# Swapping the two kinds of score products in TensorE's order, in the heads of an attention layer

## The reference

```python
q = _rope((x @ w_q.T) ...); k = _rope((x @ w_k.T) ...)     # 4 x 1024 tokens, 16 heads of 16
scores = jnp.einsum('bhqd,bhkd->bhqk', q, k) * SCALE
scores = jnp.where(tok_mask[None, None], scores, -jnp.inf)  # blocks of 64, causal
attn = jax.nn.softmax(scores, axis=-1)
ctx = jnp.einsum('bhqk,bhkd->bhqd', attn, v)
x = _layernorm(x + ctx @ w_o.T)
```

## Time and profile before

| | us |
|---|---|
| median of three runs | 1910.19 |
| lowest, highest | 1908.25, 1912.74 |
| the profiled execution's own time | 1904.56 |
| its span, first to last instruction | 1902.7 |

### The profile page before, as it was taken

How to read it: one execution, slowest core, us unless ns; L and a number is a source line. 1 busy time by engine, 2 the same in 40 slices (tenths; PEclk the granted TensorE clock), 3 DMA queues, 4 the chain that set the end, 5 groups by cost and what they waited for, 6 DMA issues and landing times.

```text
span 1902.7 us, 26419 instructions
## 1 busy us (share of the span) xinstructions
PE 1636.9 (86%) x10042; PEld 1007.7 (53%) x10043; DVE 1141.5 (60%) x2367; ACT 792.5 (42%) x1296; POOL 235.7 (12%) x237
## 2 busy tenths in 40 slices
PE   3899999986999964788899989899989899889797
PEld 3788888874558853333355433355433455433345
DVE  5556665647421144668558677568667578677465
ACT  5444444421212200437744157643167552177530
POOL 4333333311420001000000000100000100000100
PEclk8999999987999976759999989899989899988999
DMA  2000000005115502000000000000000000000000
GB/s 102 12 23 23 22 22 22 22 12 177 26 33 151 149 12 91 1 1 2 1 1 1 0 1 2 23 1 1 1 1 2 23 1 1 0 1 1 23 1 22
DMA packets 27147, 47.96 MB, mean 25 GB/s; under 512 B 7312, under 2 KB 16016, under 8 KB 26256
## 3 DMA queue, kind: packets, MB, share of 16 engines
q1 hardware_dynamic: 26464, 44.74, 7.4%
q0 software_dynamic: 576, 1.77, 0.3%
HBM read 37.59 MB, written 9.06 MB: 25 GB/s over the span
## 4 chain that ended last, share of the span: by engine, by line
issue 59%; POOL 2%; DVE 0%; POOLq 0%; DVEq 0%
POOL rs_sb L1310 1%; POOL ve_sb L1307 0%; POOL qks_sb L1325 0%; POOL v_sb L1324 0%; POOL qks_sb L1315 0%; DVE bn_sb L1489 0%; DVE x_sb_sb L1504 0%; POOLq L1144 0%; POOLq L65 0%; POOL qks_sb L1326 0%; DVE mv_sb L1495 0%; DVEq L1144 0%; POOL v_sb L1323 0%; DVEq L65 0%; DVEq L1493 0%
## 5 line engine op out<-in xcount | busy, mean ns | idle before, releaser
L1546 DVE TENSOR_REDUCE mx_sb<-s_ps 128x1 f32<-128x512 f32 (+1 forms) x512 | 313.0, 652 | 140.9 <-PE s_ps L1818 80.0
L1378 ACT ACTIVATE room_sb<-s_ps 128x1024 f32<-128x1024 f32 (+1 forms) x320 | 280.9, 950 | 21.6 <-PE s_ps L1842 20.5
L1815 PE MATMUL s_ps<-room_sb 48*128 48x512 f16 (+3 forms) x640 | 175.9, 345 | 25.1 <-DVE mx_sb L1546 16.8
L1862 PE MATMUL cm_ps<-room_sb,v_sb 128*32 128x512 f32 (+3 forms) x1536 | 167.4, 526 | 0.8 <-ACT room_sb L1384 0.8
L1842 PE MATMUL s_ps<-room_sb 51*128 51x128 f16 (+4 forms) x1152 | 123.5, 287 | 41.8 <-ACT room_sb L1378 34.9
L1307 POOL TENSOR_TENSOR ve_sb<-mv_sb,eps_sb 128x4 f32<-128x4 f32 x24 | 5.0, 210 | 1120.8 <-DVE mv_sb L1495 1120.8
L1985 PE MATMUL cm_ps<-w_fd_sb,room_sb 128*128 128x256 f32 x512 | 126.5, 394 | 14.7 <-DVE room_sb L1625 14.7
L1842 PEld LDWEIGHTS s_ps<-room_sb 50*128 50x128 f16 (+1 forms) x1152 | 39.1, 96 | 180.8 <-ACT room_sb L1378 145.0
L1815 PEld LDWEIGHTS s_ps<-room_sb 48*128 48x128 f16 x640 | 54.5, 97 | 145.8 <-DVE mx_sb L1546 97.1
L1972 PE MATMUL s_ps<-xbT_sb,w_fg_sb 128*128 128x512 f32 x256 | 128.9, 615 | 0.8 <-ACT xbT_sb L1415 0.8
L1972 PE MATMUL s_ps<-xbT_sb,w_fu_sb 128*128 128x512 f32 x256 | 127.1, 607 | 0.0
(11 more groups left out here) (242 smaller groups left out, 3250.1 us busy)
## 6 DMA issues: line engine op xcount, KB each, us to landing
we_gu_sb<-we_gu SPq DMA_DIRECT2D x32, 352.0 KB
we_dn_sb<-we_dn SPq DMA_DIRECT2D x32, 176.0 KB
x_in_sb<-x SPq DMA_DIRECT2D x9, 512.0 KB, 3.6
rows<-x_sb_sb SPq DMA_DIRECT2D x8, 512.0 KB, 3.0
x_sb_sb<-rows SPq DMA_DIRECT2D x2, 2048.0 KB, 11.5
out<-x_sb_sb SPq DMA_DIRECT2D x8, 512.0 KB, 2.6
xp_sb<-w_in SPq DMA_DIRECT2D x1, 1024.0 KB, 5.5
x_sb_sb<-w_up SPq DMA_DIRECT2D x1, 1024.0 KB, 6.6
```

The costliest lines, as they stand in the source:

```text
L1378: act.activation(weights[(g * NU + u) % SLOTS_P][:, 2 * pair:2 * pair + 2, 0:width(u) * P], W[s % 2][:, :, 0:width(u) * P], ACT.Exp, scale ...
L1546: dve.tensor_reduce(mx[:, pair, k % 2, slot:slot + 1], X[:, k % 2, 0:count * P], AX.X, ALU.max, negate=True).then_inc(mx_ok, 1)
L1815: last = pe.matmul(X[:, k % 2, at * P:(at + plain) * P], query[head:head + NORM, i * P:(i + 1) * P], key[head:head + NORM, j * P:(j + plai ...
L1862: last = pe.matmul(O[32 * h:32 * h + 32, (i - half * GT) * P:(i - half * GT + count) * P], v[:, j, g * HG + h, :], weights[(g * NU + u) % ...
```

## The change

In all steps but the first of a group, S(s + 1) used to come before M(s); now M(s) comes before S(s + 1). Step 0 had this order already. Nothing is added or removed, and no other engine's order is touched.

```diff
                         if s == 0 and g > 0:
                             weighted(b, g - 1, NU - 1, 0)
-                        if s == 0 and of < NHG:
+                        if of < NHG:
                             for_maxima(b, of, m, m + 2)
                         if s + 1 < STEPS:
                             scores(b, g, s + 1)
                         elif g + 1 < NHG:
                             scores(b, g + 1, 0)
-                        if s > 0 and of < NHG:
-                            for_maxima(b, of, m, m + 2)
                         if s == 1 and g > 0:
```

## The result

| | before | after |
|---|---|---|
| median us | 1908.99 (6 runs) | 1884.11 (6 runs) |
| lowest, highest | 1898.01, 1912.74 | 1880.26, 1888.07 |
| profiled span | 1902.7 | 1886.1 |
| mean granted clock of that execution | 0.922 | 0.927 |

The ratio is 0.9879, with a 95% interval from 0.9857 to 0.9902: 1.2% faster, some 23 us.

A forecast was written before the change was run, and what follows sets the result against it. In the heads TensorE and VectorE were taken to wait for each other, with ScalarE beside them. Gains of 1.5 + 0.3 + 0.25 us per block, times 4, made 8.2: from 1910.19 to 1902.0 us, range 1893 to 1912.

The forecast's parts named there:

- Nothing changes in a wide pair: In wide steps of the heads, 0.24 us gained and 0.23 lost per pair: zero within 0.05, period staying 3.31.
- the unseen price: Cost of S between the last half of M and W in a wide pair, taken as 0.23 us.
- the bounds: For S between M and W: from a 23 us win to a 51 us loss, over 8 pairs x 12 groups.
- rival 3: Wide pairs: S in the loop costs 0.24 us each and isn't returned, +15 us, about 1925; chance 0.14.
- The late S costs nothing: In wide steps, exponentials fed later stay hidden by VectorE's loop, with 2 us left, 1 us beside a copy.
- First groups: W(0) 1.63 us earlier: At each block's start, M(1) goes before S(2)'s wait for E(0), so W(0) comes at 837.87 instead of 839.50.
- The other groups: Start of second and third groups: M(1) no longer behind waiting S(2), so W(0) comes 0.43 us earlier.
- A part is given back at the end of a group: Late S(17) delays E(17) and W(8), leaving 0.26 us; 0.3 of 0.43 and 1.5 of 1.63 kept.
- the sum: Gains of 1.5 + 0.3 + 0.25 = 2.05 us per block, times 4 = 8.2 us.
- Rival 1: Fuller start of each block's heads brings full clock back sooner: 6 us more, about 1896; chance 0.14.

The follow-up runs named there:

- the order with two S in the loop: M before S at step 0 and the even steps only, S before M at the odd steps, against the kernel before: 1931.05 us, ratio 1.0144.
- the order with none: M before S at step 0 and the odd steps, S before M at the other even steps, against the kernel before: 1876.82 us, ratio 0.985.
- the two filled kernels: Old order and swapped order, each with unread products in TensorE's waits at the start of each block's heads, against the kernel before: ratios 0.9895 and 0.987.
- the line: Fit through 72 executions of the unchanged kernel before, time against mean clock: 1906.9 us at 0.920, less 1.60 us for each 0.001.
- the two series of runs: The swapped kernel measured against the kernel before, then once more for a second trace: 1884.11 us, ratio 0.9879, and 1885.27 us, ratio 0.9866.
- the two together: Swapped order plus unread products before the first maxima, before S(1) and behind M(1) of each first group, against the kernel before: 1880.42 us, ratio 0.987.
- The run with the early table: Swapped order plus a one-column exponential ahead of the first copy of each block's heads, against the kernel before: 1884.88 us, ratio 0.9879.
- An order that is slower by itself: M before S at all steps but step 1, against the kernel before: 1899.74 us, ratio 0.9941.

## Why the prediction was wrong, point by point

1. *Nothing changes in a wide pair.* Right. 3.31 us before and after, 1.00 from W to M and 0.54 from the last half of M to W, both as worked out. The runs with S twice and not at all in the loop gave 3.53 and 3.09, so the unseen price was 0.22 where 0.23 was taken. Both ends of its bound, nothing and 0.53, are excluded. The count of 8 such pairs in a group, in the bounds and in rival 3, was too high: the order with two S in the loop paid for six, and the order with none gained for less than one and for three in groups 1 and 2.

2. *The late S costs nothing.* Right in its result; wrong in what it would show. ScalarE's idle time before the exponentials was to grow several times and went from 21.6 to 22.2 us. The waits for S became more, 41 instead of 22, and shorter, 21.1 us together instead of 20.5, while those in front of the copies of transposes (L1368) fell from 50.7 to 36.0 us. The other way round, TensorE's waits for an exponential before S fell from 34.9 us in 84 places to 14.9 in 31.

3. *First groups: W(0) 1.63 us earlier.* Right mechanism, 1.50 measured (E(0) to W(0) 4.03 and 2.53, both at half clock): S(3) to W(0) takes 0.53 and not 0.40. At full or nearly full clock, in block 1 of the two filled kernels, it is 3.41 and 2.32, a gain of 1.1, so a part of the 1.50 is there only because the start runs at half clock. The other groups: 0.43 forecast, 0.55 measured (3.40 and 2.85).

4. *A part is given back at the end of a group.* Wrong for the most part. Groups 1 and 2 are shorter by 0.59 and 0.53, as much as W(0) is earlier, where 0.3 and 0.25 were kept in the sum. Only in the third group 0.08 goes back, from W(7) to W(8) (1.41 instead of 1.33). Sum of the order: 4 x (1.50 + 0.59 + 0.53) = 10.5 us by the groups, if the first group keeps what W(0) won; 9.0 and 8.4 by the line for the two series of runs, against 8.2 in the forecast.

5. *The step that failed: the clock had no term in the sum.* Groups 1 and 2 that ran below full clock stood in the trace, among them, and I took them for noise that "can move in either direction by some us". Rival 1 had the clock, but only behind the fuller start of a block, and with 6 us and a chance of 0.14. The runs show that the stretches inside later groups were in each of two traces before and all but gone in two after. By the line, 14 and 17 us of the gain are clock in the two series. By the traces it is 12.7 and 6.7 us in the twelve groups, beyond the 10.5 of the order, and 5.2 and 6.2 between the heads loops, of which no run shows how much belongs to the swap. The sum had nothing for any of it. So about half of the gain or more is clock, and its size is known to some us only. That the clock alone moves the time is shown by the old order with unread products (0.9895), and that it is for the most part the same time that the swap wins, by the two together (0.987). That the forecast had the direction right doesn't bear out its size: with the order alone it would have been 8 to 10 us.

What stands before such a stretch is seen in four windows of the kernel before, the 3.4 us before the clock fell in the second group of block 1 and in the third of block 3, each with those behind:

```profile
1151.30:1154.70 3.40, 2.52 (x30) 1.23 (x33) 3.02 (x9) 3.40 (x5) 0.00 (x0) 0.99 0.00 0
1154.70:1158.10 3.40, 3.40 (x19) 1.14 (x18) 1.75 (x4) 2.39 (x3) 0.00 (x0) 0.51 0.00 0
1731.50:1734.90 3.40, 2.47 (x31) 1.30 (x28) 2.48 (x6) 3.40 (x6) 0.00 (x0) 1.00 0.00 0
1734.90:1738.30 3.40, 3.40 (x22) 0.95 (x21) 2.02 (x4) 1.04 (x2) 0.00 (x0) 0.50 0.00 0
```

Here TensorE was busy 2.52 and 2.47 of 3.40 us at full clock, ScalarE all the time; then the clock is at its lower level of 1.2 GHz and TensorE busy throughout. The first lies in the middle of its group, 9 us behind E(0), the second at a group's start. The same two places of the same groups in the kernel after, and the first of them in the old order with most unread products:

```profile
1154.26:1157.66 3.40, 3.08 (x35) 1.14 (x32) 3.13 (x9) 3.40 (x6) 0.00 (x0) 1.00 0.00 0
1716.14:1719.54 3.40, 3.02 (x36) 1.61 (x36) 3.08 (x7) 3.40 (x5) 0.00 (x0) 1.00 0.00 0
1156.11:1159.51 3.40, 2.53 (x30) 1.24 (x33) 3.02 (x9) 3.40 (x5) 0.00 (x0) 1.00 0.00 0
```

The swap has TensorE busy 3.08 and 3.02 us there, half a microsecond more, and the clock stays. So the swap does change the places where it fell, in the middle of a group too. But 2.53 us in the filled kernel didn't bring it down, nor did it fall in every group of the kernel before with the same waits. What decides it was not settled; the middle of a group wasn't filled by itself, and half-clock time also came and went in code that no order touches (192.8 us before the first E(0) in both traces of before, 205.8 and 188.9 in those of after). The Trainium skill (TensorE: Matmul & The Clock Gate, Part 1: The HAM clock gate) says that activity releases the throttle. The filled runs agree, with half-clock time in the twelve groups of 9.2 us instead of 51.5 and 61.1. The run with the early table shows that less waiting at one place is no guarantee, with 43 instead of 28 us in its first groups.

## What to carry to other kernels

Read an order change twice: once as a loop of who waits for whom, where each instruction's place in the repeating part can be priced to 0.02 us, and once as a change in where TensorE idles. Groups that do the same work and differ in length by 1 to 4 us with the granted clock are a term of the sum, whose upper end is the time that they would win at full clock. Count the places where a price applies in the timeline too: the price of 0.22 us was right, the number of pairs was not. An operation that waits for one engine alone should not stand behind one that waits for another, above all where a pipeline starts; and one whose result has 1 to 2 us of slack, as S had in a wide pair, can stand behind it at no cost.

## What the runs showed of the hardware

- An order that is slower by itself (full-clock groups longer by 0.2 and 0.26 us) was faster by 0.6%, with a mean clock of 0.927 over its executions where the kernel before had 0.919.
- Products that nobody reads made the kernel 1.0% faster (ratio 0.9895), with the half-clock time in the twelve groups at 9.2 us instead of 51.5 and 61.1.
- Two products of 48 and 51 rows on different halves of the array start together, also where one is M's and the other belongs to S (925.47 and 925.48 in the wide pair above). It saved nothing: S's other head, which uses the same rows as that half of M, starts at 925.70, and W 0.31 behind it.
